# Performer features of keys and queries from two groups of 64 rows of the array, each with its own projection block and PSUM bank

## The chip, the cores and the metric

The program runs on one core of a Trainium2 chip. The metric is the device time of one execution in microseconds (us); lower is better. Five engines work side by side: TensorE (PE: matmuls, and PEld: its weight loads), VectorE (DVE), ScalarE (ACT), GpSimd (POOL) and SyncE (SP, which issues DMAs).

## What is computed

Four layers act on x of 8 x 1024 rows of 256: causal attention, an MLP with FP4 weights, a Performer block (linear attention and an MLP) and an MLP with dequantised weights. Only the linear attention of the Performer matters here. It has 16 heads of width 16 and 64 random features per head:

```python
q = split(video @ Wq.T + bq)            # 16 heads of 16
k = split(video @ Wk.T + bk)
v = split(video @ Wv.T + bv)
xp   = einsum('bhnd,md->bhnm', x * norm, proj)     # x is q or k, proj is 64 x 16
diag = sum(square(x), axis=-1, keepdims=True) * 0.5 * (norm * norm)
stab = max(xp, axis=-1)  (query)   or   max(xp, axis=(-1, -2))  (key)
feature = ratio * (exp(xp - diag - stab) + EPS_K)
ctx = einsum('bhnm,bhnd->bhmd', kp, v)
out = einsum('bhnm,bhmd->bhnd', qp, ctx) / denom[..., None]
attn = out.transpose(0, 2, 1, 3).reshape(b, n, d) @ Wo.T + bo
```

## The kernel before

Every product of full precision is made of three fp32r matmuls of high and low parts (`product`, L267: hi by hi, hi by lo, lo by hi), so `L269`, `L270` and `L271` are lines of the helper. The Performer's attention (`performer_attention`) takes one batch of 1024 rows (8 tiles of 128) at a time.

`kqT` holds the keys, later the queries, transposed: 256 values in KD = 2 chunks of 128 partitions, so a chunk holds 8 heads of 16. `proj` is block diagonal, 128 rows by 8 x 64 = 512 columns: row block h and column block h hold the 16 x 64 projection of head h. `features(i)` (L1486) makes the raw features of tile i: for each chunk c a product with 128 rows of contraction, the 128 x 128 slice of `kqT` as stationary operand and all 512 columns of `proj` as moving one, into bank c of the two banks of `ps_feat[i % 2]`. That is 6 weight loads and 6 matmuls of 512 columns per call. Each output column needs only the 16 rows of its own head; the other rows of the block are zeros.

`features` is called 16 times per batch. In the **front** of a batch (`front`, piece `f`, m = 0..7) it makes the features of the keys; ACT copies them to `kf` (L1429) and DVE takes their maxima (L1313). The front of batch b + 1 is merged with the output of batch b (`merged`) in nine slots whose pieces stand in the table `FRONT`: slot 5 has `v3 s1 f0`, slot 6 `f1 f2`, slot 7 `f3 f4`, slot 8 `f5 f6 f7`. On PE a slot is: transposes of the mixed output (L1537), 16 matmuls of the output (L1544, none in slot 8), the slot's first piece, the product with `wo` (`p_ps_b`, which waits for DVE's low part, L1337), then the other pieces. Piece f of tile m waits until ACT has copied tile m - 2 (the two buffers of `ps_feat`).

In the **tail** of a batch the maximum over all keys is made (transposed at L1565, spread over partitions at L1569, a matmul with 16 rows of contraction), the queries are projected, POOL subtracts the shift from the 8 tiles of `kf` (L1230), and PE walks over steps i: `features(i)` of the queries, the transposes of the query features of tile i - 2 (L1586), and the 16 context matmuls of tile i - 1 (L1599; the label in the trace counts two passes for each of 8). DVE, for each tile, takes the maximum of the features in PSUM (L1377), adds half the square (L1379), subtracts (L1383), and then does a share of the next batch's layer norm. `features(i)` waits for L1383 of tile i - 2, the transposes of tile i - 2 wait for ACT's exponential of it (L1463), which follows L1383.

`square_sum` has, for each chunk, the columns of the heads that the chunk's rows belong to; it is made once by POOL (L1107 to L1118). `host_layout` gives weights and biases in the layout that the kernel reads.

Of the kernel before, what the change touches and what calls it, by code (L numbers as in the profile page):

```python
# [17 lines left out]
ALU = mybir.AluOpType  # L18
# [3 lines left out]
P = 128  # L22
B, S, D = 8, 1024, 256
KD = D // P
# [249 lines left out]
def part(pair, *index):  # L274

    return tuple(a[index] for a in pair)
# [762 lines left out]
HC = HEADS // KD  # L1039


class PerformerRaw:

    FREE = 4 * KD * D
# [27 lines left out]
def performer_attention(core, dram, attn_dram, raw, mlp_raw):  # L1072
# [7 lines left out]
    with ExitStack() as ctx:  # L1080
# [17 lines left out]
        with ExitStack() as prep:  # L1098
# [3 lines left out]
            @block.gpsimd  # L1102
            def _(pool):
                pool.memset(keps[:, :], KEPS).then_inc(made, 1)
                pool.memset(ones[:, :], 1.0).then_inc(made, 1)

                pool.memset(square_sum[:, :, :], 0.0).then_inc(made, 1)  # L1107
                pool.wait_ge(made, 3)
                for c in range(KD):
                    pool.memset(square_sum[:, c, c * HC:(c + 1) * HC], 0.5 * DH ** -0.5).then_inc(made, 1)  # L1110
                pool.wait_ge(made, 3 + KD)
                for c in range(KD):
                    part_c = square_sum[:, c, c * HC:(c + 1) * HC]
                    pool.affine_select(out=part_c, in_=part_c, compare_op=ALU.is_ge, fill=0.0, base=0,
                                       pattern=[[-DH, HC]], channel_multiplier=1).then_inc(made, 1)
                    pool.wait_ge(made, 4 + KD + 2 * c)
                    pool.affine_select(out=part_c, in_=part_c, compare_op=ALU.is_ge, fill=0.0, base=DH - 1,
                                       pattern=[[DH, HC]], channel_multiplier=-1).then_inc(made, 1)  # L1118
                pool.wait_ge(made, 3 + 3 * KD)

            @block.vector
# [346 lines left out]
        def _(pe):  # L1468
# [15 lines left out]
                mm.then_inc(halfsq_done, 1)  # L1484

            def features(i):  # L1486
                for c in range(KD):
                    mm = product(pe, ps_feat[i % 2][:, c * BANK:(c + 1) * BANK],
                                 part(kqT, slice(None), c, slice(i * P, (i + 1) * P)), part(proj, slice(None)))
                return mm  # L1490

            def front(b, what, m, b_out, slot):
# [631 lines left out]
def host_layout(inputs):  # L2124
# [4 lines left out]
    def columns(v):  # L2129
        return v.reshape(-1, P).T  # L2130
# [2 lines left out]
        a[f"a_w{n}T"] = inputs[f"L0_attn_W{n}"].T  # L2133
    for n in ("gate", "up", "down"):
        a[f"f_{n}"] = inputs[f"L0_ffn_w_{n}"]
    for n in "qkvo":
        a[f"p_w{n}T"] = inputs[f"L1_attn_W{n}"].T
    for n in "kq":
        a[f"p_b{n}"] = columns(inputs[f"L1_attn_b{n}"])
    a["p_bv"] = inputs["L1_attn_bv"]  # L2140
    a["p_projT"] = inputs["L1_attn_proj"].T
    a["m_w1T"], a["m_w2T"] = inputs["L1_attn_W1"].T, inputs["L1_attn_W2"].T
# [40 lines left out]
```

## Time and profile before

| | us |
|---|---|
| median of 3 runs | 2728.48 |
| lowest, highest | 2715.63, 2732.13 |
| the profiled execution (its own time) | 2712.57 |
| its span, first to last instruction | 2710.9 |
| PE busy | 2439.4 (90%) |
| DVE busy | 1960.4 (72%) |
| ACT busy | 1196.5 (44%) |
| POOL busy | 733.1 (27%) |

The Performer's attention runs from about 1000 to 1760 us of the span: the transposes of the keys' maximum (L1565) of the eight batches start at 1049.2, 1146.4, 1243.0, 1339.7, 1434.5, 1531.7, 1626.5 and 1721.3 us, so a batch takes 94.7 to 97.2 us.

How to read it: a matmul's busy time is longer than the time it keeps the array from the next, because matmuls overlap; what a matmul costs in a stream is the distance from its start to the next one's start. In rows of the timeline the first column is the start in us from the span's start, the second how long the merged group of instructions took in us, then engine, line, operation, output and inputs, for matmuls the active rows*columns of the array and the shape of the output, and the count; in brackets the engine's idle time before it and what ended it. "PEclk" is the granted TensorE clock as a share of full speed: 1.0 is 2.4 GHz, 0.5 is 1.2 GHz.

### The profile page before, as it was taken

What the parts mean: (1) busy time and instruction counts of PE and PEld (TensorE: products, weight loads), DVE (VectorE), ACT (ScalarE), POOL (GpSimd) and SP (SyncE); (2) the same over time, 40 slices, a digit from 0 to 9 for tenths busy, and PEclk for the clock granted to TensorE, in tenths of its full rate; (3) what the DMA queues carried; (4) which work ended last, traced back from release to release, by engine and by line L of the source; (5) the groups of instructions that cost most, each with busy time, mean ns of one, the idle gap of its engine ahead of it and who ended that gap; (6) DMA issues with size and microseconds to landing.
All of it is one profiled execution on the core that took longest, in us unless ns stands there. A gap on an engine that the chain in (4) does not pass through costs nothing. (4 is left out here: it accounts for less than half of the span.)

```text
span 2710.9 us, 44219 instructions
## 1 busy us (share of the span) xinstructions
PE 2439.4 (90%) x16012; PEld 2226.7 (82%) x16012; DVE 1960.4 (72%) x3617; ACT 1196.5 (44%) x1864; POOL 733.1 (27%) x452
## 2 busy tenths in 40 slices
PE   7999996889998969999999999958888888799999
PEld 6888885888888868898898899847777777699998
DVE  5666675899999966566566656648999998866664
ACT  4444543343344325445456445523333333444444
POOL 1111111444444433123212312214344442211110
PEclk9999998899999989999999999968999989899999
DMA  5000000000000000000000000020000010100000
GB/s 168 0 0 0 0 0 19 1 1 0 0 0 0 1 16 1 16 8 8 15 12 4 15 15 8 9 67 24 17 24 15 15 39 1 41 17 23 23 23 32
DMA packets 43114, 45.94 MB, mean 17 GB/s; under 512 B 2976, under 2 KB 42016, under 8 KB 42784
## 3 DMA queue, kind: packets, MB, share of 16 engines
q1 hardware_dynamic: 43040, 44.95, 5.3%
q8 instruction: 47, 0.77, 0.1%
q14 instruction: 27, 0.22, 0.0%
HBM read 28.16 MB, written 16.78 MB: 17 GB/s over the span
## 5 line engine op out<-in xcount | busy, mean ns | idle before, releaser
L1738 ACT ACTIVATE m_a<-m_ps_wide,m_b 128x512 f32<-128x512 f32 x128 | 88.4, 691 | 286.4 <-PE m_ps_wide L271 198.6
L1706 PE MATMUL m_ps_z<-m_w_hi,m_a_hi 128*128 128x256 f32 x512 | 152.5, 298 | 53.9 <-DVE m_a_lo L1778 53.8
L1738 ACT ACTIVATE d_a<-d_ps_wide,d_b 128x512 f32<-128x512 f32 x128 | 88.3, 690 | 190.4 <-PE d_ps_wide L271 188.4
L1778 DVE TENSOR_TENSOR d_a_lo<-d_a,d_a_hi 128x512 fp32r<-128x512 f32 x128 | 86.8, 690 | 110.7 <-ACT d_a_hi L1742 109.7
L1230 POOL TENSOR_TENSOR p_kf<-p_kf,p_k_shift 128x1024 f32<-128x1024 f32 x64 | 119.4, 1903 | 155.5 <-DVE p_k_shift L1364 155.5
L1706 PEld LDWEIGHTS m_ps_z<-m_w_hi,m_a_hi 128*128 128x128 f32 x512 | 102.4, 200 | 68.6 <-DVE m_a_lo L1778 63.5
L1706 PE MATMUL m_ps_z<-m_w_lo,m_a_hi 128*128 128x256 f32 x512 | 149.5, 292 | 0.0
L1706 PE MATMUL m_ps_z<-m_w_hi,m_a_lo 128*128 128x256 f32 x512 | 149.2, 291 | 0.0
L1706 PE MATMUL d_ps_z<-d_w_hi,d_a_lo 128*128 128x256 f32 x512 | 145.4, 284 | 0.0
L1706 PE MATMUL d_ps_z<-d_w_lo,d_a_hi 128*128 128x256 f32 x512 | 145.0, 283 | 0.0
L1706 PE MATMUL d_ps_z<-d_w_hi,d_a_hi 128*128 128x256 f32 x512 | 143.9, 281 | 0.3 <-DVE d_a_lo L1778 0.3
L269 PE MATMUL f_ps_gate<-f_gate_w_hi,f_n_T_hi 128*128 128x352 f32 x256 | 93.6, 366 | 39.6 <-ACT f_silu L942 39.6
L1313 DVE TENSOR_REDUCE p_kmax<-p_kf 128x16 f32<-128x1024 f32 x64 | 78.1, 1220 | 65.4 <-ACT p_kf L1429 65.0
L194 POOL TENSOR_TENSOR f_h_q<-f_h_q,f_h_scale 128x1408 f32<-128x1408 f32 x32 | 83.2, 2599 | 155.5 <-DVE f_h_q L191 155.5
L1544 PE MATMUL p_ps_a<-p_ctx_pair,p_kf 128*128 128x34 f32 x1024 | 123.6, 277 | 0.0
L1544 PEld LDWEIGHTS p_ps_a<-p_ctx_pair,p_kf 128*128 128x128 f32 x1024 | 122.7, 196 | 0.4
L1599 PEld LDWEIGHTS p_ps_a<-p_v,p_kf 128*128 128x128 f32 x1024 | 120.2, 192 | 0.8
L1599 PE MATMUL p_ps_a<-p_v,p_kf 128*128 128x34 f32 x1024 | 119.8, 272 | 0.0
L269 PE MATMUL m_ps_wide<-m_h_hi,m_w_hi 128*128 128x512 f32 x256 | 109.0, 426 | 3.8 <-DVE m_h_lo L1771 3.7
L1937 DVE SCALAR_TENSOR_TENSOR m_o<-m_o,m_o_mean,m_g 128x256 f32<-128x256 f32 x64 | 111.9, 1807 | 0.0
L269 PE MATMUL p_ps_feat<-p_proj_hi,p_kqT_hi 128*128 128x512 f32 x256 | 111.7, 436 | 0.0
L1463 ACT ACTIVATE raw_weights<-raw_weights 128x1024 f32<-128x1024 f32 x64 | 67.8, 1060 | 98.5 <-DVE raw_weights L1383 98.5
(342 smaller groups left out, 8707.9 us busy)
## 6 DMA issues: line engine op xcount, KB each, us to landing
residual<-in_x SPq DMA_DIRECT2D x8, 1024.0 KB, 11.8
attn<-p_attn SPq DMA_DIRECT2D x32, 256.0 KB, 2.1
m_attn<-attn SPq DMA_DIRECT2D x16, 512.0 KB, 3.8
out<-residual SPq DMA_DIRECT2D x16, 512.0 KB, 2.9
raw_weights<-in_d_q SPq DMA_DIRECT2D x2, 1024.0 KB, 7.2
d_scale<-in_d_scale SPq DMA_DIRECT2D x2, 1024.0 KB, 6.0
raw_weights<-in_m_w1T SPq DMA_DIRECT2D x1, 1024.0 KB, 4.9
raw_weights<-in_m_w2T SPq DMA_DIRECT2D x1, 1024.0 KB, 9.4
```

Of the source, the lines that this page charges most:

```text
L194: return pool.tensor_tensor(self.blocked(v), self.blocked(v), self.spread(self.scale[slot][:, :]), ALU.mult)
L269: pe.matmul(out, lhsT[0], rhs[0], start=start, stop=False)
L1230: pool.tensor_tensor(f, f, k_shift[:, i, :].unsqueeze(2).broadcast_to([P, HEADS, M]), ALU.subtract).then_inc(k_shifted, 1)
L1313: small_k.add(dve.tensor_reduce(kmax[:, m, :], kf[:, m, :].rearrange("p (h m) -> p h m", h=HEADS), AX.X, ALU.max))
L1463: act.activation(qf[i % 2][:, :], qf[i % 2][:, :], ACT.Exp).then_inc(q_exp, 1)
L1544: mm = pe.matmul(ps_a[:, k * 2 * VW:(k + 1) * 2 * VW], qfT[:, i, k, :], ctx_pair[:, k, :], start=True, stop=True)
L1599: mm = pe.matmul(ps_a[:, k * 2 * VW:(k + 1) * 2 * VW], kf[:, j, k * P:(k + 1) * P], vt[:, k * 2 * VW:(k + 1) * 2 * VW], start=False, stop= ...
L1706: mm = pe.matmul(z, a, w[:, f, :], start=(f == 0 and k == 0 and j % 2 == 0), stop=(f == FC - 1 and k == 2), skip_group_check=True)
L1738: act.activation(self.a[f % RING][:, :], self.ps_wide[f % 2][:, :], self.func, bias=self.b1[:, f:f + 1])
L1778: dve.tensor_tensor(self.a2[1][:, f, :], self.a[f % RING][:, :], self.a2[0][:, f, :].bitcast(F32), ALU.subtract).then_inc(self.a_lo, 1)
L1937: o_tally.add(dve.scalar_tensor_tensor(o[:, j, :], o[:, j, :], o_moments.mean[:, j:j + 1], g3[:, :], ALU.subtract, ALU.mult))
```

## The change

`features` splits each chunk's 128 partitions into two groups of 64 rows (4 heads each). Each group multiplies its 64 rows of `kqT` with its own 64 x 256 block of `proj` and writes its own bank of `ps_feat[i % 2]`: group r goes to bank r, chunk c to its columns c*256 onwards. A call has 12 weight loads and 12 matmuls of 256 columns and 64 rows in place of 6 and 6 of 512 columns and 128 rows. The two groups alternate, so that neighbours use different rows of the array and different banks. The zero blocks that are left out are those between the two groups.

So that the heads come out in the old order, the rows of Wk, Wq and their biases are permuted by the host (`by_row_group`), and `square_sum`'s blocks are laid to match, with as many instructions as before. Wv and Wo are as before.

```diff
+RG = 64
+GROUPS, HR = P // RG, RG // DH
...
+                def heads_of(c):
+                    return square_sum[:, c, :].rearrange("p (r k l) -> p r k l", r=GROUPS, k=KD)[:, :, c, :]
+
                 for c in range(KD):
-                    pool.memset(square_sum[:, c, c * HC:(c + 1) * HC], 0.5 * DH ** -0.5).then_inc(made, 1)
+                    pool.memset(heads_of(c), 0.5 * DH ** -0.5).then_inc(made, 1)
...
             def features(i):
+                hi, lo = kqT
+                n = HR * M
                 for c in range(KD):
-                    mm = product(pe, ps_feat[i % 2][:, c * BANK:(c + 1) * BANK],
-                                 part(kqT, slice(None), c, slice(i * P, (i + 1) * P)), part(proj, slice(None)))
+                    for k, (a, w) in enumerate(((hi, proj[0]), (hi, proj[1]), (lo, proj[0]))):
+                        for r in range(GROUPS):
+                            rows, at = slice(r * RG, (r + 1) * RG), r * BANK + c * n
+                            mm = pe.matmul(ps_feat[i % 2][:, at:at + n], a[rows, c, i * P:(i + 1) * P],
+                                           w[rows, r * n:(r + 1) * n], start=(k == 0), stop=(k == 2))
                 return mm
...
-    for n in "qkvo":
+    def by_row_group(v):
+        return v.reshape(GROUPS, KD, HR * DH, -1).transpose(1, 0, 2, 3).reshape(v.shape)
+
+    for n in "vo":
         a[f"p_w{n}T"] = inputs[f"L1_attn_W{n}"].T
     for n in "kq":
-        a[f"p_b{n}"] = columns(inputs[f"L1_attn_b{n}"])
+        a[f"p_w{n}T"] = by_row_group(inputs[f"L1_attn_W{n}"]).T
+        a[f"p_b{n}"] = columns(by_row_group(inputs[f"L1_attn_b{n}"]))
```

On PE, a step of the tail before (names: `p_ps_feat` the raw features, `p_ps_turn` the transposed query features, `p_ps_a` the context):

```order
L269 MATMUL p_ps_feat<-p_proj_hi,p_kqT_hi 128x512
L270 MATMUL p_ps_feat<-p_proj_lo,p_kqT_hi 128x512
L271 MATMUL p_ps_feat<-p_proj_hi,p_kqT_lo 128x512
L269 MATMUL p_ps_feat<-p_proj_hi,p_kqT_hi 128x512
L270 MATMUL p_ps_feat<-p_proj_lo,p_kqT_hi 128x512
L271 MATMUL p_ps_feat<-p_proj_hi,p_kqT_lo 128x512
L1586 MATMUL p_ps_turn<-ident,raw_weights 128x128 x8
```

and the same place with the change:

```order
L1500 MATMUL p_ps_feat<-p_proj_hi,p_kqT_hi 128x256 x2
L1500 MATMUL p_ps_feat<-p_proj_lo,p_kqT_hi 128x256 x2
L1500 MATMUL p_ps_feat<-p_proj_hi,p_kqT_lo 128x256 x2
L1500 MATMUL p_ps_feat<-p_proj_hi,p_kqT_hi 128x256 x2
L1500 MATMUL p_ps_feat<-p_proj_lo,p_kqT_hi 128x256 x2
L1500 MATMUL p_ps_feat<-p_proj_hi,p_kqT_lo 128x256 x2
L1598 MATMUL p_ps_turn<-ident,raw_weights 128x128 x8
```

Nothing else moved: each matmul became a pair at the same place, and the transposes behind them stand where they stood. Every other engine has the same instructions in the same order.

## Rows read from the trace of the kernel before

**Rows 1.** Busy time by window, the Performer stage: busy (count) per engine, PEclk, DMA.

```profile
1000.00:1760.00 760.00, 731.67 (x5077) 660.99 (x5075) 467.70 (x808) 397.20 (x536) 178.74 (x137) 0.97 0.03 11
```

**Rows 2.** Groups by form, PE: line, names, stationary rows*columns, output, count, busy, mean.

```profile
L269 PE MATMUL p_ps_feat<-p_proj_hi,p_kqT_hi 128*128 128x512 f32 x256 | 111.7, 436 | 0.0
```

**Rows 3.** Timeline, PE, one step of the tail: start, length (us), instruction.

```profile
1173.56 0.48 PE L269 MATMUL p_ps_feat<-p_proj_hi,p_kqT_hi 128*128 128x512 f32 x1
...
1175.03 1.03 PE L1586 MATMUL p_ps_turn<-ident,raw_weights 128*128 128x128 f32 x8
1175.90 1.87 PE L1599 MATMUL p_ps_a<-p_v,p_kf 128*128 128x34 f32 x16
1177.61 0.48 PE L269 MATMUL p_ps_feat<-p_proj_hi,p_kqT_hi 128*128 128x512 f32 x1
```

**Rows 4.** Timeline, PE, first and last of 12 products of 256 columns in a row.

```profile
1109.91 0.28 PE L269 MATMUL p_ps_feat<-p_wv_hi,p_nT_hi 128*128 128x256 f32 x1
...
1111.21 0.28 PE L271 MATMUL p_ps_feat<-p_wv_hi,p_nT_lo 128*128 128x256 f32 x1
```

**Rows 5.** Timeline, PEld (weight loads), features of queries.

```profile
1160.68 0.19 PEld L271 LDWEIGHTS p_ps_feat<-p_proj_hi,p_kqT_lo 128*128 128x128 f32 x1
1160.91 0.19 PEld L269 LDWEIGHTS p_ps_feat<-p_proj_hi,p_kqT_hi 128*128 128x128 f32 x1
```

**Rows 6.** Timeline, PE, the only matmuls of 16 rows in the stage.

```profile
1148.45 0.39 PE L1569 MATMUL p_ps_b<-p_stab_diag,p_ones 16*128 16x16 f32 x2 [0.27 <-DVE p_stab_diag L1360]
1148.77 0.50 PE L269 MATMUL p_ps_feat<-p_nT_hi,p_wq_hi 128*128 128x512 f32 x1
```

**Rows 7.** Timeline, PE, slots 7 and 8 of the front.

```profile
1131.43 0.38 PE L1537 MATMUL p_ps_b<-ident,p_mixed 128*128 128x128 f32 x2
...
1134.82 0.28 PE L269 MATMUL p_ps_b<-p_wo_hi,p_mixedT_hi 128*128 128x256 f32 x1
...
1136.68 0.39 PE L271 MATMUL p_ps_feat<-p_proj_hi,p_kqT_lo 128*128 128x512 f32 x1
...
1139.77 0.38 PE L269 MATMUL p_ps_b<-p_wo_hi,p_mixedT_hi 128*128 128x256 f32 x1 [1.09 <-DVE p_mixedT_lo L1337]
...
1140.59 0.41 PE L269 MATMUL p_ps_feat<-p_proj_hi,p_kqT_hi 128*128 128x512 f32 x1
...
1146.38 0.27 PE L1565 MATMUL p_ps_b<-ident,p_kmax_all 128*16 128x128 f32 x1
```

**Rows 8.** Timeline, ACT and DVE, the same stretch.

```profile
1137.11 1.03 ACT L1429 ACTIVATE p_kf<-p_ps_feat 128x1024 f32<-128x1024 f32 x1 [0.79 <-PE p_ps_feat L271]
1143.56 1.03 ACT L1429 ACTIVATE p_kf<-p_ps_feat 128x1024 f32<-128x1024 f32 x1 [0.35 <-PE p_ps_feat L271]
...
1138.17 1.22 DVE L1313 TENSOR_REDUCE p_kmax<-p_kf 128x16 f32<-128x1024 f32 x1 [0.87 <-ACT p_kf L1429]
1139.30 0.41 DVE L1337 TENSOR_TENSOR p_mixedT_lo<-p_ps_b,p_mixedT_hi 128x256 fp32r<-128x256 f32 x1
```

**Rows 9.** Timeline, DVE, one step of the tail.

```profile
1175.23 1.23 DVE L1377 TENSOR_REDUCE p_q_shift<-p_ps_feat 128x16 f32<-128x1024 f32 x1 [0.55 <-PE p_ps_feat L271]
...
1179.28 1.22 DVE L1377 TENSOR_REDUCE p_q_shift<-p_ps_feat 128x16 f32<-128x1024 f32 x1 [0.39 <-PE p_ps_feat L271]
```

**Rows 10.** Timeline, DVE beside POOL, start of two batches' tails.

```profile
1157.10 1.74 DVE L1379 TENSOR_TENSOR p_q_shift<-p_q_shift,p_halfsq_q 128x16 f32<-128x16 f32 x1
...
1542.02 0.31 DVE L1379 TENSOR_TENSOR p_q_shift<-p_q_shift,p_halfsq_q 128x16 f32<-128x16 f32 x1
...
1549.13 0.65 DVE L1379 TENSOR_TENSOR p_q_shift<-p_q_shift,p_halfsq_q 128x16 f32<-128x16 f32 x1
...
1534.81 14.93 POOL L1230 TENSOR_TENSOR p_kf<-p_kf,p_k_shift 128x1024 f32<-128x1024 f32 x8 [20.56 <-DVE p_k_shift L1364]
```

**Rows 11.** Windows at the start of two batches' tails.

```profile
1154.00:1158.00 4.00, 4.00 (x12) 3.15 (x12) 2.37 (x3) 0.00 (x0) 4.00 (x3) 0.60 0.00 0
1347.00:1351.00 4.00, 4.00 (x24) 3.42 (x23) 2.47 (x4) 0.00 (x0) 4.00 (x3) 1.00 0.00 0
```

More of the change, by code:

```diff
@@ L1108, in _ @@
                 pool.wait_ge(made, 3)
+                def heads_of(c):
+                    return square_sum[:, c, :].rearrange("p (r k l) -> p r k l", r=GROUPS, k=KD)[:, :, c, :]
                 for c in range(KD):
-                    pool.memset(square_sum[:, c, c * HC:(c + 1) * HC], 0.5 * DH ** -0.5).then_inc(made, 1)
+                    pool.memset(heads_of(c), 0.5 * DH ** -0.5).then_inc(made, 1)
                 pool.wait_ge(made, 3 + KD)
                 for c in range(KD):
-                    part_c = square_sum[:, c, c * HC:(c + 1) * HC]
-                    pool.affine_select(out=part_c, in_=part_c, compare_op=ALU.is_ge, fill=0.0, base=0,
-                                       pattern=[[-DH, HC]], channel_multiplier=1).then_inc(made, 1)
+                    pool.affine_select(out=heads_of(c), in_=heads_of(c), compare_op=ALU.is_ge, fill=0.0, base=0,
+                                       pattern=[[-RG, GROUPS], [-DH, HR]], channel_multiplier=1).then_inc(made, 1)
                     pool.wait_ge(made, 4 + KD + 2 * c)
-                    pool.affine_select(out=part_c, in_=part_c, compare_op=ALU.is_ge, fill=0.0, base=DH - 1,
-                                       pattern=[[DH, HC]], channel_multiplier=-1).then_inc(made, 1)
+                    pool.affine_select(out=heads_of(c), in_=heads_of(c), compare_op=ALU.is_ge, fill=0.0, base=DH - 1,
+                                       pattern=[[RG, GROUPS], [DH, HR]], channel_multiplier=-1).then_inc(made, 1)
                 pool.wait_ge(made, 3 + 3 * KD)
```

## The prediction, made before the changed kernel ran

> **What bounds the kernel now.** I first looked at busy time by window. The Performer stage has PE at work for 731.67 of 760 us at a mean granted clock of 0.97, DVE for 468 and ACT for 397 [rows 1]. The view by groups shows the features there: three groups of 256 matmuls of 512 columns with all 128 rows, of which one is shown [rows 2]. Then the timeline gives what a matmul costs in the stream. In the queries' features the weight loads, one per matmul, start 0.23 us apart [rows 5], so a call of six keeps PE 1.38 us; behind small matmuls its first weight load is not hidden and it takes 1175.03 - 1173.56 = 1.47 us [rows 3]. Products of 256 columns start (1111.21 - 1109.91) / 11 = 0.118 us apart [rows 4]. The 16 context matmuls of 34 columns take 1177.61 - 1175.90 = 1.71 us [rows 3], 0.107 us each although they stream almost nothing: that is the rate of weight loads of 128 columns. So at 256 columns the streaming and the weight load are worth the same, about 0.11 us, and this is what the change turns on.
>
> A step of the tail takes 4.05 us on PE [rows 3]. In the same step DVE has 0.39 us to spare [rows 9], so its floor is 4.05 - 0.39 = 3.66 us. PE sets the pace, DVE is close behind.
>
> **The change, part by part.**
>
> *One call.* It removes 6 matmuls of 512 columns (1.38 us) and adds 12 of 256. Three prices are possible. If both groups load and stream at the same time, a pair costs what one full 256-column matmul costs: 6 x 0.118 = 0.71 us. If they take turns, 12 x 0.118 = 1.42 us. If only the streaming is shared but the loads take turns, 12 x 0.107 = 1.28 us plus what does not overlap, so about 1.3 to 1.4 us. No matmul in this trace uses one half of the rows beside the other half, so no row decides it. What speaks for the first: the two groups read different partitions and write different banks, and rows 5 and 3 show that PE already starts a weight load while the matmul before it, of the same rows, still runs (the matmuls last 0.39 us [rows 7], loads follow every 0.23). I take 0.71 us, with 1.42 as the other bound.
>
> *Change of mode.* The features now use 64 rows, all their neighbours 128. The nearest rows are the matmuls of 16 rows: the two matmuls of L1569 and the way back to 128 rows take 1148.77 - 1148.45 = 0.32 us [rows 6], where 2 x 0.107 = 0.21 would do. So a change of mode costs about 0.1 us; going in and out is 0.2 us a call. The bounds are 0 (hidden by the queue) and 0.2 each.
>
> The Trainium skill (TensorEngine Tiling (Array Packing), Key Properties) says that tiles can load weights and multiply in parallel, and that a change of tiling mode drains the engine. The second half agrees with the 0.1 us of rows 6; the first is what no row here shows.
>
> So a call falls from 1.38 to 0.71 + 0.2 = 0.91 us: 0.47 us saved where PE sets the pace.
>
> *The front of a batch* (seven are merged with an output). f0 saves 0.47 us. In slots 6 and 7 the first piece (f1, f3) stands ahead of the product with `wo`, which waits for a chain: the features before it end on PE, ACT copies them (1.03 us), DVE reduces them (1.22), then makes the low part (0.41) [rows 8]. That chain is seen bare in slot 8: f4 ends at 1136.68 + 0.23 = 1136.91, the product starts at 1139.77 after 1.09 us of idleness [rows 7], so it is 2.86 us. In slot 7 PE itself took 1134.82 - 1131.43 = 3.39 us for this stretch [rows 7]; less 0.47 it is 2.92, still above 2.86. So f1 and f3 save 0.47 each, hardly more even if the price were lower; f2 and f4 save 0.47 each; f5 saves nothing, it stands under the chain already. f6 and f7 end in the maximum over all keys. Now f6 starts at 1140.59, the copy of f7 at 1143.56, and the maximum is turned at 1146.38 [rows 7, 8]. Then f6 is done at 1140.59 + 0.91 + about 0.1 = 1141.6, two copies in a row end at 1143.66 instead of 1144.59, and DVE, which must reduce two tiles of 1.22 us back to back, gives back some 0.2: 0.75 us saved. Sum 5 x 0.47 + 0.75 = 3.1 us, times 7 = 21.7. The first batch's front has no output beside it, and its eight calls go from 1.38 to DVE's 1.22 us each: 8 x 0.16 = 1.3, I take 1.
>
> *The tail of a batch* (eight). At its start POOL subtracts in 8 pieces, 14.93 us in all, 1.87 us each, and DVE's tiny addition L1379 lasts until POOL's piece ends: 0.31, 0.65, even 1.74 us [rows 10], to about 1549.8 in the sixth batch. While this holds, DVE's steps are tied to POOL's pieces and nothing is saved. After it four steps are PE's: features 4 to 7, one at 0.47 and three capped by DVE's floor at 0.39: 1.6 us x 8 = 12.8.
> In five batches of eight the first two calls of the tail ran at a granted clock of about 0.5 to 0.6, in the others at 1.0 (one of each kind shown) [rows 11]. There tile 0 came too late for a POOL piece, and L1379 took 1.74 instead of 0.31 us [rows 10]: 1.4 us. A call shorter by 0.5 us or more catches that piece: 5 x 1.4 = 7.
>
> *Layout.* POOL's six instructions on `square_sum` are as many as before and run before the stage; weights are permuted on the host. Nothing.
>
> Sum: 21.7 + 1 + 12.8 + 7 = 42.5 us. Against the profiled execution's 2712.57 this gives 2670. The median of the runs shown stands 15.9 us above that execution, which would give 2686; their lowest stands 3 above. I forecast the middle, 2678.
>
> **The rivals.**
>
> *The groups take turns, no gain (B).* 1.42 + 0.2 = 1.62 us a call, 0.24 more than now. About 11 calls a batch are at PE's pace (8 in the front less f5, 4 in the tail): 0.24 x 11 x 8 = 21 us, 2734 on the profile, 2750 on the median. For it: weight loads are the limit at 0.107 us in rows 3 whatever is streamed, and the change doubles their number. If there is one path for weights, halving the columns streamed brings nothing.
> The Trainium skill (TensorE: Matmul & The Clock Gate, Part 3) says that weight loads overlap running matmuls only when the row group differs; by this, one group's load and matmul are in series while the other's run beside it, 0.107 + 0.107 = 0.21 us a pair and again no gain. Its first half is not what the loads of full rows show here, which start every 0.23 us under matmuls that last 0.39.
>
> *Part of the loads overlaps (B').* A pair at 0.14 to 0.2 us: from 1.04 to 1.4 us a call with the changes of mode, saving 0 to 0.34: 2680 to 2728. A saving of 27 us (1%) needs 0.31 us a call, so a pair at or below 0.145 us.
>
> *Slower: every change of group costs a change of mode (C).* Neighbours in a call now differ in their rows. If each costs the 0.1 us of rows 6, a matmul costs 0.22 us and a call 2.6 us, 1.24 more; 15 of 16 calls show it (f5 has cover), 1.24 x 15 x 8 = 149 us: 2862 on the profile, 2877 on the median. It decides from a mean of 0.125 us per matmul upwards (0.31 us a call, 27 us in all). Against it: rows 6 shows the cost between different heights of the array, not between two places of the same height.
>
> *The clock (D).* The clock fell in five tails behind the 32 matmuls of 16 columns [rows 11]. If PE with half its rows in each matmul is granted the lower clock, a call of 0.91 us becomes about 1.8, 0.9 more; with half of the 11 x 8 calls at PE's pace in such stretches that is 40 us, the whole gain (2710 on the profile), with all of them 2750.
>
> **How the numbers follow.** Full overlap (A) 0.50, B 0.27, B' 0.10, C 0.08, D 0.05. About 1% (27 us) is what a measurement tells from no change. A alone: 2663 on the profile if changes of mode are free (0.67 a call: 5 x 0.53 + 0.9 in the front, capped by the chain; 1.84 in the tail; 9 from POOL's pieces; 50 in all), 2697 on the median if each costs 0.2; its own range is 2655 to 2700. The whole range must reach B's 2750, which leaves out C and half of D: 2652 to 2750. Faster by over 1%: A but for its upper edge, and half of B', 0.52. Within 1%: most of B and half of B', 0.32. Slower: C, D and the edge of B, 0.16.
>
> **What would show it.** In the profile after, pairs of 256-column matmuls at L1500 starting 0.12 us apart per pair, a call of about 0.9 us, and tail steps of 3.66 with DVE no longer idle: A. Starts 0.12 us apart per matmul, steps of 4.2 or more: B. 0.2 per matmul: C. The chain into the product with `wo` stays 2.86 us in slot 8; if slots 6 and 7 show idleness there of more than 0.1 us, PE fell further than I took. I would be wrong on size if L1379 stays at 1.74 us in half of the tails, or if PEclk falls below 0.97 over the stage.

## The result, and the profile after

The changed kernel takes 2852.8 us (median of 4; 2835.72 to 2920.42) against 2726.95 for the kernel before: a ratio of 1.045, 95% interval [1.039, 1.051]. The forecast was 2678, at most 2750. The profiled execution is the slowest of the four, with a mean granted clock of 0.867 against 0.884 to 0.898 for the others, so the lengths of its instructions can be read but its totals overstate the loss.

From the page of the changed kernel: span, busy time, the granted clock in 40 slices of the span, and the queue that brings code.

```profile
span 2918.7 us, 45755 instructions
PE 2613.2 (90%) x16780; PEld 2410.3 (83%) x16780; DVE 1967.9 (67%) x3617; ACT 1199.6 (41%) x1864; POOL 733.5 (25%) x452
PEclk9999997999999877586768867765899999799999
q8 instruction: 102, 1.67, 0.2%
```

The clock is at 5 to 8 tenths in slices 15 to 28, which are 1022 to 2043 us: that is the Performer's attention. PE has 174 us more busy time (2439.4 before) although its work shrank. From the first transposes of the stage to its end it took 783.6 us before and 990.9 now: 207 more, as much as the whole difference of the two profiled executions (2920.42 - 2712.57 = 208). So the rest of the program lost nothing.

Windows of the kernel before and then of the changed one, both from the first to the last maximum over all keys, which is seven whole batches (span, busy and count of PE, PEld, DVE, ACT, POOL, then PEclk, DMA share, GB/s):

```profile
1049.00:1721.00 672.00, 658.45 (x4628) 597.45 (x4627) 411.35 (x722) 353.08 (x484) 153.51 (x112) 0.98 0.03 11
```

```profile
1046.00:1900.00 854.00, 805.95 (x5299) 752.13 (x5300) 418.49 (x721) 355.88 (x483) 153.43 (x112) 0.73 0.03 10
```

Multiply length and PEclk and you have the stretch in microseconds of full clock: 659 before, 854 x 0.73 = 623 after. (PEclk has two digits, so this is good to some 4 us; DVE and ACT do not follow this clock, so it is a rough measure.) Counted so, the change saves 36 us. It is the clock, from 0.98 to 0.73, that turns the saving into a loss. (A kernel below, with the same matmuls in another order, took 2848.92 us and has 807 us at 0.78 in this window: the same picture, less overstated.)

**At full clock the parts came as forecast.** Timeline of the changed kernel, PE, a step of the fifth batch's tail (its maximum is at 1555.7):

```profile
1585.48 0.39 PE L1500 MATMUL p_ps_feat<-p_proj_hi,p_kqT_hi 64*128 64x256 f32 x2
1585.71 0.28 PE L1500 MATMUL p_ps_feat<-p_proj_lo,p_kqT_hi 64*128 64x256 f32 x2
...
1586.39 1.09 PE L1598 MATMUL p_ps_turn<-ident,raw_weights 128*128 128x128 f32 x8
1587.32 1.87 PE L1611 MATMUL p_ps_a<-p_v,p_kf 128*128 128x34 f32 x16
1589.12 0.39 PE L1500 MATMUL p_ps_feat<-p_proj_hi,p_kqT_hi 64*128 64x256 f32 x2
```

Each row is a pair, one matmul of either group. A call takes 1586.39 - 1585.48 = 0.91 us where [rows 3] has 1.47, a step 3.64 where it had 4.05. DVE has become the bound in it. Timeline of the changed kernel, DVE, the same place:

```profile
1586.50 1.22 DVE L1384 TENSOR_REDUCE p_q_shift<-p_ps_feat 128x16 f32<-128x1024 f32 x1
1587.76 0.17 DVE L1386 TENSOR_TENSOR p_q_shift<-p_q_shift,p_halfsq_q 128x16 f32<-128x16 f32 x1
```

No idle time stands in brackets at the maximum, where [rows 9] has 0.39 us.

**In the low stretches everything on PE takes twice as long.** A step in the fourth batch's tail of the same execution:

```profile
1454.80 0.58 PE L1500 MATMUL p_ps_feat<-p_proj_hi,p_kqT_hi 64*128 64x256 f32 x2
1455.17 0.42 PE L1500 MATMUL p_ps_feat<-p_proj_lo,p_kqT_hi 64*128 64x256 f32 x2
...
1456.38 1.97 PE L1598 MATMUL p_ps_turn<-ident,raw_weights 128*128 128x128 f32 x8
1458.14 3.47 PE L1611 MATMUL p_ps_a<-p_v,p_kf 128*128 128x34 f32 x16
1461.54 0.58 PE L1500 MATMUL p_ps_feat<-p_proj_hi,p_kqT_hi 64*128 64x256 f32 x2
```

The call takes 1.58 us, the transposes 1.76, the context matmuls 3.40, the step 6.74. The 16 context matmuls, whose price is that of their weight loads, go from about 0.11 to 0.21 us each: the loads became slower by the same factor. Windows of the changed kernel around this tail (the maximum of the batch is at 1429.84):

```profile
1423.00:1430.00 7.00, 4.71 (x13) 3.42 (x13) 0.75 (x1) 1.27 (x2) 0.00 (x0) 0.52 0.00 0
1450.00:1501.00 51.00, 51.00 (x259) 49.63 (x260) 22.08 (x46) 21.18 (x24) 1.65 (x1) 0.50 0.00 1
1501.00:1528.00 27.00, 27.00 (x219) 25.74 (x217) 10.69 (x22) 8.35 (x17) 2.94 (x4) 0.99 0.06 21
```

In the second window PE is busy in 51 of 51 us and is granted 0.50, which is 1.2 of 2.4 GHz. Of its 259 matmuls 128 have 34 columns (context and the first outputs of the next slots), 74 are transposes, and 48 are tiled features; of the rest, six matmuls with `wo` and three of a projection have 256 and 512 columns on all 128 rows. In the third window, with projections and products with `wo` all along, the clock is back (0.99). From maximum to maximum the batches take 128.0, 128.9, 126.9, 125.9, 98.8, 126.9 and 118.6 us, where before they took 94.7 to 97.2.

**A second loss was in no case of the prediction.** Timeline of the changed kernel, PE, the end of a front:

```profile
1542.55 0.38 PE L269 MATMUL p_ps_b<-p_wo_hi,p_mixedT_hi 128*128 128x256 f32 x1 [1.43 <-DVE p_mixedT_lo L1344]
...
1544.85 0.28 PE L1500 MATMUL p_ps_feat<-p_proj_hi,p_kqT_lo 64*128 64x256 f32 x2
1548.38 0.49 PE L269 MATMUL p_ps_feat<-p_nT_hi,p_wq_hi 128*128 128x512 f32 x1 [3.26 <-issue]
...
1551.32 0.79 PE L271 MATMUL p_ps_feat<-p_nT_hi,p_wq_lo 128*128 128x512 f32 x1 [2.21 <-issue]
```

And the waits of the changed kernel, PE, in the stage (us in total, times, longest):

```profile
PE p_ps_feat L269 <- issue: 18.9, 6, 3.4
PE p_ps_feat L271 <- issue: 13.7, 6, 2.7
```

Before the first projection of the queries PE waits 3.26 us and a little later 2.21, for nothing that the profile shows; this comes in six of the batches, and the trace of before has no such wait. The instruction queue moved 102 packets, 47 before; between the first and the last maximum 60, where before has 6. A pass of the loop over batches holds 661 matmuls on PE before and 757 now, each with its weight load, since a call has 12 and not 6. So I took these waits to be PE's code arriving late, and tested that below. The packets themselves bear it out: in the packed trace a packet of this queue (16 KB) ends inside each of these twelve waits, and the wait is over 1.4 to 1.7 us later. For the two waits shown, packets end at 1546.87 and 1549.94, and PE goes on at 1548.38 and 1551.32. The low clock comes with them (0.52 in the window before the maximum, where the wait stands).

### The profile page after: what moved, and what is told of

Same layout as the page of the kernel before. It is cut to its first block and busy times, and to the rows that moved or that the text cites. A ratio compares the mean times of both kernels' runs of the same rounds, so it can differ in the third digit from the quotient of the medians.

```text
span 2918.7 us, 45755 instructions
## 1 busy us (share of the span) xinstructions
PE 2613.2 (90%) x16780; PEld 2410.3 (83%) x16780; DVE 1967.9 (67%) x3617; ACT 1199.6 (41%) x1864; POOL 733.5 (25%) x452
## 5 line engine op out<-in xcount | busy, mean ns | idle before, releaser
L1611 PEld LDWEIGHTS p_ps_a<-p_v,p_kf 128*128 128x128 f32 x1024 | 201.5, 299 | 1.3
L1611 PE MATMUL p_ps_a<-p_v,p_kf 128*128 128x34 f32 x1024 | 197.1, 367 | 0.0
L1556 PEld LDWEIGHTS p_ps_a<-p_ctx_pair,p_kf 128*128 128x128 f32 x1024 | 157.9, 243 | 0.0
L1556 PE MATMUL p_ps_a<-p_ctx_pair,p_kf 128*128 128x34 f32 x1024 | 156.7, 318 | 0.0
L1384 DVE TENSOR_REDUCE p_q_shift<-p_ps_feat 128x16 f32<-128x1024 f32 x64 | 78.0, 1219 | 93.7 <-PE p_ps_feat L1500 93.7
L1467 ACT ACTIVATE p_kf<-p_ps_turn 128x1024 f32<-128x1024 f32 x64 | 65.3, 1020 | 150.6 <-PE p_ps_turn L1598 150.6
L1598 PE MATMUL p_ps_turn<-ident,raw_weights 128*128 128x128 f32 x512 | 117.9, 407 | 3.3 <-ACT p_kf L1467 3.3
L1296 DVE SCALAR_TENSOR_TENSOR p_kqT_lo<-p_ps_feat,raw_weights,p_kqT_hi 128x512 fp32r<-128x512 f32 x64 | 48.0, 751 | 106.4 <-ACT p_squares L1423 106.4
```

Source lines behind the costliest of these rows:

```text
L1384: small_t.add(dve.tensor_reduce(q_shift[:, s, :], f, AX.X, ALU.max))
L1467: act.activation(kf[:, i - 2, :], ps_turn[:, :], ACT.Copy, bias=KEPS).then_inc(qfT_ready, 1)
L1556: mm = pe.matmul(ps_a[:, k * 2 * VW:(k + 1) * 2 * VW], qfT[:, i, k, :], ctx_pair[:, k, :], start=True, stop=True)
L1598: mm = pe.transpose(ps_turn[:, k * P:(k + 1) * P], qf[i % 2][:, k * P:(k + 1) * P], ident[:, :])
L1611: mm = pe.matmul(ps_a[:, k * 2 * VW:(k + 1) * 2 * VW], kf[:, j, k * P:(k + 1) * P], vt[:, k * 2 * VW:(k + 1) * 2 * VW], start=False, stop= ...
```

## Experiments

The letters in the expectations name the theories: W, the clock falls because fewer columns are streamed, whatever the rows; H, because matmuls on 64 rows bring the low clock by themselves; M, because of the changes between 64 and 128 rows; R, a later one, because fewer rows times columns are streamed; L, the longer body of the loop makes PE wait for its code. Diffs are against the changed kernel unless said otherwise. For each kernel the window from first to last maximum is shown.

### The tail's calls alone, the front's calls alone

```diff
-            def features(i):
+            def features(i, of):
+                if of != TILED:
+                    for c in range(KD):
+                        mm = product(pe, ps_feat[i % 2][:, c * BANK:(c + 1) * BANK],
+                                     part(kqT, slice(None), c, slice(i * P, (i + 1) * P)), part(proj, slice(None)))
+                    return mm
```

`TILED` is "q" in the first, "k" in the second; `square_sum` and the layout of the weights are made for keys and queries apart.

> Only the queries' features (the tail of a batch) by two row groups, the keys' as before. After the change the clock fell at the start of the tail's features and rose in the projections of the next front. Every theory: PEclk falls in the tail and the first part of the next front, and stays 1.0 in the slots with the keys' features; over the stage about 0.85, time 2760 to 2800. If the two halves of the change only together pull the clock down, PEclk stays above 0.93 and the time is about 2700.

> Only the keys' features (the front of a batch) by two row groups, the queries' as before. W: the front's slots 6 to 8 have more other full matmuls beside the features, so the clock falls there in part of the time only; PEclk about 0.9, time 2720 to 2760. H and M: the same fall as in the whole change at these slots, and it lasts until the tail. If the tail alone is the cause: PEclk 0.96 and about 2690 us (22 us from the front).

Tail only: 2813.18 us, ratio 1.035 [1.029, 1.041]. Front only: 2707.73, 0.993 [0.990, 0.997]. First the tail's kernel, then the front's:

```profile
1050.00:1795.00 745.00, 728.52 (x4963) 675.23 (x4963) 413.99 (x722) 353.50 (x484) 153.44 (x112) 0.85 0.03 10
```

```profile
1050.00:1712.00 662.00, 643.62 (x4963) 588.40 (x4962) 413.81 (x721) 351.50 (x482) 153.38 (x112) 0.97 0.03 11
```

The same count of matmuls, but the clock is 0.85 in one and 0.97 in the other. So the long low stretches come from the tail's calls. This is the last case of the second expectation, whose clock (0.96) is met; the time is 18 us above its 2690. The front-only kernel is faster than the kernel before, but by a small 0.7%; the tail-only kernel is slower than the 2760 to 2800 that was expected. Neither has the waits before the projections, with 709 matmuls in a pass of the loop.

### Whether the groups overlap

```diff
-                    for k, (a, w) in enumerate(((hi, proj[0]), (hi, proj[1]), (lo, proj[0]))):
-                        for r in range(GROUPS):
+                    for r in range(GROUPS):
+                        for k, (a, w) in enumerate(((hi, proj[0]), (hi, proj[1]), (lo, proj[0]))):
```

> The changed kernel with the two row groups in turns of three matmuls instead of one by one, so that neighbours mostly use the same 64 rows. If neighbours of the same rows do not overlap, a call takes 10 or more times 0.118 us, about 1.3 us. Theory W: the columns per time are those of before, so PEclk is back near 0.97 and the time about 2735 us. Theory H: half of the array works in each matmul, PEclk stays low (0.75 or less) and the time is over 2900. Theory M: as many changes of mode as after the change, PEclk about 0.75 and over 2850.

2848.92 us, 1.044 [1.037, 1.052], like the changed kernel. Its window is like that too, 807 x 0.78 = 629 us in full clock:

```profile
1046.00:1853.00 807.00, 759.49 (x5302) 706.37 (x5301) 418.96 (x723) 354.74 (x483) 153.42 (x112) 0.78 0.03 10
```

The reason is in the timeline of this kernel, PE and then PEld:

```profile
1400.74 0.39 PE L1500 MATMUL p_ps_feat<-p_proj_hi,p_kqT_hi 64*128 64x256 f32 x2
1400.96 0.28 PE L1500 MATMUL p_ps_feat<-p_proj_lo,p_kqT_hi 64*128 64x256 f32 x2
```

```profile
1400.74 0.19 PEld L1500 LDWEIGHTS p_ps_feat<-p_proj_hi,p_kqT_hi 64*128 64x128 f32 x2
1400.84 0.20 PEld L1500 LDWEIGHTS p_ps_feat<-p_proj_lo,p_kqT_hi 64*128 64x128 f32 x2
```

The program issues three matmuls of group 0 and then three of group 1; the trace shows them still in pairs, x2, one of each group. PE had let the second group's past those of the first. So the experiment didn't make what it was to make, groups that take turns, and tells nothing on the price of turns. It does show the overlap from another side. The Trainium skill (TensorE: Matmul & The Clock Gate, Part 3) says that matmuls start and end strictly in the order of the program; for matmuls of different row groups this trace says otherwise: group 1's first starts 10 ns after group 0's first, ahead of group 0's second and third.

### Less work on full rows

Against the kernel before; three of six matmuls are left out of every call.

```diff
             def features(i):
-                for c in range(KD):
-                    mm = product(pe, ps_feat[i % 2][:, c * BANK:(c + 1) * BANK],
-                                 part(kqT, slice(None), c, slice(i * P, (i + 1) * P)), part(proj, slice(None)))
-                return mm
+                at, of = slice(i * P, (i + 1) * P), ps_feat[i % 2]
+                pe.matmul(of[:, 0:BANK], kqT[0][:, 0, at], proj[0][:, :], start=True, stop=False)
+                pe.matmul(of[:, 0:BANK], kqT[0][:, 0, at], proj[1][:, :], start=False, stop=True)
+                return pe.matmul(of[:, BANK:2 * BANK], kqT[0][:, 1, at], proj[0][:, :], start=True, stop=True)
```

> The kernel before, full rows, but each call of features leaves out three of its six matmuls (both products with low parts of the second chunk, and the keys' low part of the first), so a call has 3 x 512 columns and takes about 0.7 us like the overlapped pairs of the change, with no half-row matmul. Theory W (the clock falls because the array streams fewer columns in the same time, whatever took them away): PEclk over the Performer stage falls from 0.97 to about 0.75 as after the change, and the time is 2800 to 2900 us. Theory H (matmuls on 64 rows bring the low clock by themselves) and theory M (the changes between 64 and 128 rows do): PEclk stays at 0.97 and the time falls by 40 to 50 us, to about 2675.

2736.19 us, 1.004 [1.002, 1.006]: half of the feature matmuls are gone and nothing is gained.

```profile
1050.00:1740.00 690.00, 665.40 (x4293) 606.08 (x4292) 414.03 (x721) 352.07 (x482) 153.53 (x112) 0.86 0.03 11
```

No matmul of half height is in it, and the clock is 0.86 all the same. So neither H nor M can be the whole cause: leaving out full matmuls is enough to bring low stretches. But W's figures (about 0.75 and 2800 to 2900 us) are missed as well. In microseconds of full clock this is 690 x 0.86 = 593, 66 fewer than before.

### Half rows without the overlap

All 12 matmuls of a call go to the same 64 rows, so the outputs are not the heads'.

```diff
-                            rows, at = slice(r * RG, (r + 1) * RG), r * BANK + c * n
+                            rows, at = slice(0, RG), r * BANK + c * n
...
-                                           w[rows, r * n:(r + 1) * n], start=(k == 0), stop=(k == 2))
+                                           w[rows, 0:n], start=(k == 0), stop=(k == 2))
```

> The changed kernel with all twelve matmuls of a call on the same 64 rows (partitions 0 to 63, projection columns 0 to 255): the outputs of the features are not those of the heads, but sizes, banks and order are the same. Nothing can overlap, a call takes 12 x 0.118 + 0.2 = 1.6 us and streams as long as before the change, always with half of the rows. W: no long low stretches, PEclk over the stage 0.95 or more, time about 2735 us. H: long low stretches as after the change, time above 2900. M: the same as H.

3142.96 us, 1.155 [1.151, 1.159]. Window, and then two rows of its timeline, PE:

```profile
1064.00:2118.00 1054.00, 1043.08 (x5297) 982.22 (x5296) 416.29 (x721) 358.95 (x482) 153.31 (x112) 0.61 0.02 8
```

```profile
1500.48 0.63 PE L1500 MATMUL p_ps_feat<-p_proj_hi,p_kqT_lo 64*128 64x256 f32 x2
1500.91 0.62 PE L1500 MATMUL p_ps_feat<-p_proj_hi,p_kqT_hi 64*128 64x256 f32 x2
```

A call streams as many columns as before, one matmul after the other (0.21 us each, at low clock), and PE is busy in 99% of the window, yet the clock is 0.61. W expected 0.95 or more here, since the columns are those of before; so W is not the whole cause either. Changes of mode are in it too, but the next experiment shows that these alone leave the clock at 0.97. Taken with the previous experiment: a kernel with half of the feature matmuls and a kernel with all of them on half of the rows both show the low clock. This kernel also shows what a pair costs without overlap: 2 x 0.21 us at low clock, against 0.21 to 0.22 for the pair in the changed kernel's low step.

### The change of mode alone

Against the kernel before; one small matmul of 64 rows is added ahead of each call.

```diff
             def features(i):
+                pe.matmul(ps_feat[i % 2][:, 0:16], kqT[0][0:64, 0, i * P:(i + 1) * P], proj[0][0:64, 0:16], start=True, stop=True)
                 for c in range(KD):
```

> The kernel before with one small matmul (64 rows, 16 columns, overwritten by what follows) ahead of the six of each call: two changes of mode a call and nothing else of the change. By the 0.1 us of the rows before, a change in and out and the small matmul cost about 0.3 us a call, some 12 of 16 calls on the path: 25 to 35 us, 2750 to 2760. M: long low stretches appear, over 2800. W and H: PEclk over the stage stays at 0.95 or more.

2773.72 us, 1.020 [1.016, 1.023]. Window and a step of the tail, PE:

```profile
1054.00:1771.00 717.00, 709.74 (x4740) 632.66 (x4739) 418.57 (x722) 353.55 (x484) 153.50 (x112) 0.97 0.03 10
```

```profile
1392.95 1.87 PE L1600 MATMUL p_ps_a<-p_v,p_kf 128*128 128x34 f32 x16
1394.75 0.27 PE L1487 MATMUL p_ps_feat<-p_proj_hi,p_kqT_hi 64*128 64x16 f32 x1
1394.95 0.50 PE L269 MATMUL p_ps_feat<-p_proj_hi,p_kqT_hi 128*128 128x512 f32 x1
...
1396.45 1.03 PE L1587 MATMUL p_ps_turn<-ident,raw_weights 128*128 128x128 f32 x8
```

The context matmuls and the way into the mode take 1.80 us (1.71 in [rows 3]), the call with the small matmul 1.70 (1.47). That is 0.32 more: 0.11 for the matmul, if it costs what one of 34 columns does [rows 3], and so about 0.1 for each change of mode. Over 16 calls in seven batches it makes 36 us; the window has 717 x 0.97 = 695 in full clock, 36 more than before. The clock stays at 0.97, so in the kernel with all its full matmuls the changes of mode alone don't lower it, against M. The time is above the 2750 to 2760 that was expected. The window is 45 us longer than that of before: some 31 to 36 are these calls, and the rest is the clock, for the short low stretches after the maxima are 48 us in all where before has 21.

### Work put back into the tail

```diff
-            def features(i):
+            def features(i, fillers):
...
+                for z in range(fillers):
+                    pe.matmul(ps_feat[i % 2][:, z * BANK:(z + 1) * BANK], hi[:, 0, i * P:(i + 1) * P], proj[0][:, :],
+                              start=True, stop=True)
```

`fillers` is 2 in the tail, 0 in the front; what they write is overwritten by the call.

> The changed kernel, but each of the eight calls in the tail has two more matmuls ahead of its twelve, of full rows and 512 columns, whose result is overwritten. A tail call takes 0.71 + 0.2 + 2 x 0.23 = 1.37 us again, with six pairs of half rows and their changes of mode as in the change. W (too few columns streamed per time): the array streams 0.43 us more per call, the low stretches of 50 to 75 us from the tail into the next front go away or become rare, PEclk over the stage above 0.92, time 2700 to 2735. H (half rows) and M (changes of mode): the stretches stay, about as long as in the tail-only kernel (300 us in the stage), time 2800 or more.

2767.1 us, 1.018 [1.013, 1.024].

```profile
1046.00:1765.00 719.00, 677.16 (x5412) 604.94 (x5411) 410.50 (x722) 353.86 (x483) 153.47 (x112) 0.92 0.04 12
```

Sixteen useless matmuls more per batch make the kernel 2.7% faster than the changed one (1.018 against 1.045, some 73 us). Of the low stretches over 10 us one is left, of 24 us; the changed kernel has them in six of seven batches. The clock came as W had it, 0.92; the time is above its 2700 to 2735. The waits before the projections stayed, 30.3 us in all, with 773 matmuls in a pass of the loop.

### Full rows in the tail, as many instructions as the changed kernel

```diff
-                            rows, at = slice(r * RG, (r + 1) * RG), r * BANK + c * n
+                            rows = slice(r * RG, (r + 1) * RG) if groups else slice(None)
+                            at = r * BANK + c * n
```

`groups` is true in the front only. The tail's 12 matmuls of 256 columns now use 128 rows each.

> The changed kernel, but the calls of the tail use all 128 rows in each of their twelve matmuls of 256 columns (same banks, same columns, same count of instructions): the front is by two groups, the tail streams what it streamed before. Theory R (the clock goes by rows times columns streamed): no long low stretches in the tail, since a call streams 12 x 256 columns of full rows again. Theory L (a loop body that is longer by 192 instructions on PE makes it wait for its code once per batch, 5.5 us in all ahead of the queries' projections, at which the clock falls too): those waits and the low stretch at -7 to 0 us before the maximum stay. Both together: about 8 us per batch more than the front-only kernel, 2760 to 2775. If the waits had come from the half rows, they go: 2710.

2749.97 us, 1.010 [1.007, 1.013].

```profile
1046.00:1747.00 701.00, 656.62 (x5298) 616.42 (x5299) 410.90 (x721) 352.71 (x483) 153.37 (x112) 0.94 0.04 12
```

Its waits in the stage, PE, and its instruction queue:

```profile
PE p_ps_feat L269 <- issue: 18.5, 6, 3.5
PE p_ps_feat L271 <- issue: 12.2, 6, 2.6
```

```profile
q8 instruction: 102, 1.67, 0.3%
```

The clock is back to 0.94. The only edit against the changed kernel is the rows of the tail's matmuls (with them go the overlap and the changes of mode there), and the waits are unchanged, within 0.1 us in the longest. So they do not come from the half rows or the low clock of the tail. The front-only kernel differs from this one by 48 matmuls in a pass of the loop; its instruction queue, for comparison:

```profile
q8 instruction: 48, 0.79, 0.1%
```

From 709 to 757 matmuls the packets double and the waits appear; between the first and the last maximum the queue moved 5 packets in the front-only kernel and 60 in this one. Between 2707.73 (0.993) and 2749.97 (1.010) lie about 1.7%, some 46 us (the two intervals leave 34 to 58), which I put down to the code: 5.5 us of waiting in most batches, and the low stretch of 6.8 us beside it. Twelve matmuls of 256 columns for six of 512 are 0.04 us a call, 3 us in all, of it. The time is below the 2760 to 2775 that was expected.

### Is it the work or the rows that count in the tail?

Against the kernel before, in calls of the tail only (the front's stay whole). The first leaves out three of six matmuls. The second, whose diff this is, does too, and has in addition the small matmul of 64 rows and 16 columns, which the first lacks.

```diff
-            def features(i):
+            def features(i, half):
+                if half:
+                    at, of = slice(i * P, (i + 1) * P), ps_feat[i % 2]
+                    pe.matmul(of[:, 0:16], kqT[0][0:64, 0, at], proj[0][0:64, 0:16], start=True, stop=True)
+                    pe.matmul(of[:, 0:BANK], kqT[0][:, 0, at], proj[0][:, :], start=True, stop=False)
+                    pe.matmul(of[:, 0:BANK], kqT[0][:, 0, at], proj[1][:, :], start=False, stop=True)
+                    return pe.matmul(of[:, BANK:2 * BANK], kqT[0][:, 1, at], proj[0][:, :], start=True, stop=True)
```

> The kernel before, full rows, front as before, but the tail's calls leave out three of their six matmuls (as in the half-work kernel). The counterpart of the tail-only kernel, which streams 12 x 256 columns by 64 rows: the same rows times columns. R: the same long low stretches as there in about half of the batches (200 to 300 us in the stage) and about its time, 2790 to 2820, less the 0.2 us of mode changes per call. If half rows weigh more than half work: low for less than 100 us, time about 2715.

> The kernel with half of the work in the tail's calls (three full matmuls of six are left out), and one small matmul of 64 rows and 16 columns, overwritten, ahead of them: full rows, half work, and two changes of mode a call, so that a call takes about the 0.9 to 1.0 us of a call by two groups. It tells why the tail-only kernel (2813 us) lost more to the clock than the tail with half work (2747). If the changes of mode and the longer call weigh in the clock: low stretches of 50 us and more as in the tail-only kernel, 2800 or more. If half rows weigh more than half work by themselves: low stretches of 27 us at most as without the small matmul, 2750 to 2765.

The first: 2746.9 us, 1.010 [1.007, 1.014]; low stretches of at most 27 us, batches of 93.1 to 104.8. The second: 2774.53, 2790.49, 2828.65 and 2871.38 us, too wide a spread for a ratio, against 2714.39 for before beside it. Its profiled execution (2790.49) has low stretches of 68 us in two batches and of 10 to 31 in three more, batches of 93.4 to 122.7.

```profile
1049.00:1743.00 694.00, 672.21 (x4460) 612.50 (x4459) 415.19 (x722) 352.45 (x484) 153.47 (x112) 0.91 0.03 11
```

```profile
1049.00:1788.00 739.00, 726.42 (x4516) 661.32 (x4515) 416.00 (x722) 353.53 (x484) 153.62 (x112) 0.86 0.03 10
```

In its profiled execution the second has nearly the clock and the time of the tail-only kernel's profiled one (0.86 and 2790.49 against 0.85 and 2794.34). Its two lowest times are 2.2 and 2.8% above before, where the tail-only kernel stands at 3.5% [2.9, 4.1]. So half the work alone gives about a third of that loss, and the 0.3 us that the small matmul and its two changes of mode add to each call bring it most of the way. Whether the tiled matmuls add something beyond this is not shown: four times that spread over 97 us can't tell. Both expectations of the first are missed: its time lies between R's 2790 to 2820 and the other case's 2715.

### Filling the front's own gap

Against the front-only kernel: two matmuls of 512 columns are put before the small ones with 16 rows (L1569 in the kernel before). In the front-only kernel the clock still falls for some microseconds after each maximum, as in the kernel before [rows 11].

```diff
                 project("q", 2)
+                for z in range(2):
+                    pe.matmul(ps_feat[1][:, BANK:2 * BANK], w["q"][0][:, 0, 0:P], nT[0][:, 0, 0:BANK], start=True, stop=True)
                 pe.wait_ge(stab_ready, b + 1)
```

> The front-only kernel with two full matmuls of 512 columns (overwritten) in the gap of 0.46 us ahead of the matmul that spreads the shift, to see whether more columns just ahead of the 32 small matmuls keep the clock there. If so, the low stretch of 6.8 us at 6.3 to 13.1 us after the maximum goes, 2 to 3 us a batch, and the time is 2685 to 2695; if not, 2705 to 2715 as without them.

2711.1 us, 0.998 [0.995, 1.000]. The twelve times fall in two groups, 2698 to 2709 and 2713 to 2724, so it is not shown to be better or worse than the front-only kernel, and this front with its extra matmuls is not shown to beat the kernel before. The low stretch went, as hoped, and yet the time is not the 2685 to 2695 that should have followed.

```profile
1048.00:1697.00 649.00, 633.36 (x4975) 580.74 (x4976) 408.62 (x721) 351.69 (x483) 153.41 (x112) 0.99 0.03 11
```

It is useful for one thing: five of its seven batches take 92.0 us and have no low stretch; the best of before take 94.7. Against 659 before, 649 x 0.99 = 643 in full clock.

## Why the prediction was wrong, step by step

**The call, right.** 6 x 0.118 + 0.2 = 0.91 us was taken, 0.91 measured. The pair at 0.118 us is case A; case B would be twice that, as the one-group kernel shows at low clock (0.42 for two matmuls, where the changed kernel's pair takes 0.21). Behind small matmuls the call was 1.47 before and not 1.38, so in the tail it saved 0.56 us, of which DVE let 0.41 show. The Trainium skill (TensorEngine Tiling (Array Packing), Key Properties) says that tiles load and multiply in parallel; the trace agrees, with the loads of the two groups 3 ns apart in the changed kernel (1585.477 and 1585.480 us in the packed trace) and the next pair's 0.11 to 0.12 us later.

**The changes of mode, right.** 0.1 us each, as [rows 6] gave it, shown by the kernel with nothing else in it.

**The tail's step at full clock, right.** 3.66 was taken from DVE's spare time, 3.64 measured, with DVE no longer idle.

**The front, right.** In slot 8 the features end at 1539.56 + 0.12 = 1539.68 and the product starts at 1542.55: a chain of 2.87 us, taken as 2.86. Slots 6 and 7 show no idleness there. The gain per batch was taken as 3.1 us; the batches with no low stretch in the last experiment show 94.7 - 92.0 = 2.7. The front-only kernel gained 0.7% [0.3, 1.0], about 18 us, of the 22.7 for all fronts.

**The pieces of POOL, wrong and small.** I took 7 us from L1379 catching an earlier piece in five tails. That was read from one row: of the five tails with the low clock only the second has 1.74 us, the others 0.19, 0.81, 0.51 and 0.74, so the term was too large from the start. Then the line's mean went from 316 ns to 418 (64 instructions): 6.5 us more, not less. Its first instruction takes 1.60 to 1.96 us in five tails of the changed kernel, which was a sign of being wrong that the prediction had named.

**The clock, the step that failed.** The sum has no term for the clock: it books 12.8 and 7 us of savings in the tail as if PE kept the clock of before. The prediction looked at the low clock in [rows 11] and made a rival of it, D, at 0.05. Two things were wrong with it. First the chance: I asked only whether half rows might count less, and did not ask what PE would still be streaming once the calls had shrunk. The rows had it: in a step of 4.05 us [rows 3] the features' 1.47 were the only full streaming, 1.71 are matmuls of 34 columns. A tail cut to 3.64 us by cutting just that part streams hardly anything, and the five low starts of tails in [rows 11] lay behind another run of small matmuls. Then the size: I let the calls alone become slower, by 0.9 us each, which with all calls gave 2750. In the low stretches everything on PE is, the context matmuls alone by 1.6 us a step, and the stretch lasts 50 to 70 us, into the next front. The tail-only kernel measures +3.5%, about 94 us more, where the prediction had 12.8 us saved and 7 more from POOL's pieces. The clock over the whole window fell from 0.98 to 0.73, the other sign that the prediction had named. D's own reason, half rows, is borne out in part: the one-group kernel streams as many columns as before and has 0.61, but the kernels with half the work on full rows fall to 0.86 and 0.91 without it.

**The code, not in the prediction at all.** It priced the added instructions by their time on the array alone, and so put at nothing what it takes to bring them. By the comparison above it costs some 46 us.

The parts add up: -0.7% (front) + 3.5% (tail) + 1.7% (code) = 4.5%, the 1.045 that was measured. That this sum is so close is partly luck, for each term has an interval of 0.3 to 0.6% to either side, and it takes the losses as independent, which no run tests.

**What stays open.** Low stretches some 20 to 27 us before the maximum, inside the front, stand in most batches of the changed kernel and in three of that with fillers, not in the front-only one, though their fronts are the same. In the front-only kernel and most others a low stretch of about 70 us covers the end of the Performer stage and the start of the next, where before has 44, which eats some 10 us of the gain; why is not known. Where between 709 and 757 matmuls the code waits begin was not looked for. The first of the two waits lies beside the 256 KB that the output writes, and its packet takes 1.3 to 2.1 us where that of the second wait takes 0.9 to 1.2; whether this transfer lengthens it wasn't tried. How the chip decides on the clock is not shown here, only in which streams it fell.

## What to carry to other kernels

Before shortening the matmuls of a stretch, look at what PE streams between them. Here the rest was small matmuls that weight loads pace; with the big ones cut, a step that should have gone from 4.05 to 3.64 us became one of 6.74 in most tails, and useless big ones brought more than half of the loss back. Row groups gained a little where the neighbours stream full matmuls (here the front) and lost much where they don't. Compare versions by length times granted clock to see which part is work and which is clock. And count a loop body's instructions when an edit doubles some of them: the instruction queue's packets, and waits for "issue" at a fixed place of each pass, tell when it has grown too long.

## What the runs showed of the hardware

- Two groups of 64 rows load and multiply at the same time: a pair of 256-column matmuls every 0.118 us, the price of one of 128 rows [rows 4].
- PE takes a matmul of the other row group ahead of earlier ones: issued as three and three, they ran in pairs, 10 ns apart.
- Going into or out of 64-row mode cost 0.1 us each way: a step with one small matmul of 64 rows is 0.32 us longer.
- PE can be busy without a gap at 1.2 GHz: 51 of 51 us at 0.50. With the features' matmuls on the same 64 rows, one after another, PE was busy for 99% of the window and its mean clock 0.61.
- At the low clock weight loads were slower by the same factor: 16 loads and small matmuls took 3.40 us, not 1.71 to 1.80.
- A loop body of 757 matmuls and their loads waited about 5.5 us in most passes, one of 709 did not (102 and 48 packets of instructions in the whole run). In the changed kernel each wait ended 1.4 to 1.7 us after a packet of the instruction queue did.
